# An image network on one core: layers 0 and 1 held as 4 rows x 32 channels, with the input turned by VectorE and the column transform first

## The reference, cut to what matters

```python
# layer 0: whole image moved down and right by (dy, dx), found from its own mean; cut at the border
offsets = clip(mean_feat @ W + b, 0, 28).astype(int32)
x = x + where(mask, gn(x)[b, i - dy, j - dx, :], 0)
# layer 1: 3x3 convolution of signs with summed signs of weights
x = x + conv(sign(gn(x)), sign(W).sum(axis=0), 'SAME') + b.sum(axis=0)
# layers 2 and 3: cosine transform along columns, real Fourier transform along rows, 32 x 32 modes kept,
# each mode times a 32 x 32 complex matrix R, and back; beside it a 32 x 32 channel matrix
v = einsum('kn,bcxn->bcxk', D, gn(x)); v = rfft(v, axis=-2, norm='ortho')[..., :32, :32]
u = irfft(einsum('ijab,ejab->eiab', R, v), n=224); v_out = einsum('kn,bcxk->bcxn', D, u)
x = x + relu(v_out + gn(x) @ W.T + b)
```

## Time and profile before

| | |
|---|---|
| median of 3 runs | 3808.79 us (3801.92 to 3814.15) |
| profiled execution | 3800.75 us, span 3798.7 us |
| TensorE busy, share of the span | 2990.2 us, 79% |
| VectorE | 2738.1 us, 72% |
| ScalarE | 1522.8 us, 40% |
| first stage (to the last instruction of its last image) | about 0 to 1818 us |
| mixing, layer 2 | 1820 to 1955 us |
| third layer | 1955 to 3085 us |
| mixing, layer 3 | 3085 to 3222 us |
| last layer | 3222 us to the end |

### The profile page before, as it was taken

How to read it: one execution, slowest core, us unless ns; L and a number is a source line. 1 busy time by engine, 2 the same in 40 slices (tenths; PEclk the granted TensorE clock), 3 DMA queues, 4 the chain that set the end, 5 groups by cost and what they waited for, 6 DMA issues and landing times. The chain is left out here.

```text
span 3798.7 us, 64095 instructions
## 1 busy us (share of the span) xinstructions
PE 2990.2 (79%) x20528; PEld 1622.4 (43%) x20528; DVE 2738.1 (72%) x4615; ACT 1522.8 (40%) x3060; POOL 36.9 (1%) x23
## 2 busy tenths in 40 slices
PE   2688888888888888888348787887878735999997
PEld 2455555555554555544243333333333315444443
DVE  2566666666566666665537889989898744899998
ACT  3477766666677766655312222222222213000000
POOL 0000000000000000000100000000000010000000
PEclk9799998999899998989658899898898965999998
DMA  4566765666666675653657757767576353999998
GB/s 121 160 196 191 207 203 169 183 177 187 173 194 177 199 207 169 184 163 110 137 150 222 234 196 224 219 213 226 191 243 192 141 120 103 345 387 386 383 386 296
DMA packets 244496, 793.86 MB, mean 209 GB/s; under 512 B 41706, under 2 KB 76190, under 8 KB 233396
## 3 DMA queue, kind: packets, MB, share of 16 engines
q1 hardware_dynamic: 172692, 473.01, 42.4%
q10 hardware_dynamic: 70912, 316.72, 23.7%
q0 software_dynamic: 608, 0.63, 0.1%
HBM read 464.31 MB, written 329.10 MB: 209 GB/s over the span
## 5 line engine op out<-in xcount | busy, mean ns | idle before, releaser
L1307 ACT ACTIVATE B_junk<-B_im,B_nk 128x896 bf16<-128x896 f32 x224 | 233.4, 1042 | 855.9 <-DVE B_im L1377 659.0
L1253 PE MATMUL B_ring<-B_im,B_wnorm 128*128 128x448 f32 x896 | 413.3, 605 | 157.7 <-DVE B_im L1347 155.9
L755 DVE SCALAR_TENSOR_TENSOR A_image<-A_cps,A_cbias,A_image 128x448 f32<-128x448 f32 x448 | 303.3, 681 | 226.8 <-PE A_cps L415 200.8
L1576 PE MATMUL C_ring<-C_im,C_wnorm 128*128 128x448 f32 x896 | 387.8, 571 | 24.4 <-DVE C_ubuf L1633 19.0
L415 PE MATMUL A_cps<-A_signa,A_cwa 128*64 128x448 bf16 x1344 | 354.1, 378 | 63.9 <-DVE A_signa L781 43.0
L373 PE MATMUL A_aps<-a_k_ident,A_tin 112*128 112x112 f32 x1792 | 274.8, 297 | 108.2 <-ACT A_image L525 72.3
L415 PE MATMUL A_cps<-A_signb,A_cwb 128*64 128x448 bf16 x1344 | 354.8, 378 | 0.0
L547 ACT ACTIVATE A_tout<-A_aps 112x512 f32<-112x512 f32 x448 | 242.4, 591 | 266.4 <-PE A_aps L426 266.1
L1253 PEld LDWEIGHTS B_ring<-B_im,B_wnorm 128*128 128x128 f32 x896 | 172.9, 204 | 402.7 <-issue 334.5
L1225 PE MATMUL B_ring<-B_rout,iB_k_rowf 128*64 128x512 f32 x896 | 269.3, 684 | 76.4 <-DVE B_rout L1370 76.1
L749 DVE SCALAR_TENSOR_TENSOR A_image<-A_sps,A_lin,A_image 128x448 f32<-128x448 f32 x448 | 304.4, 682 | 13.4 <-PE A_sps L373 3.2
(11 more groups left out here) (195 smaller groups left out, 4023.9 us busy)
## 6 DMA issues: line engine op xcount, KB each, us to landing
A_tin<-in_x SPq DMA_DIRECT2D x441, 448.0 KB, 4.9
B_rin<-x2s SPq DMA_DIRECT2D x1024, 112.0 KB, 3.4
x2s<-A_tout ACTq DMA_DIRECT2D x224, 448.0 KB, 4.4
x3s<-B_im ACTq DMA_DIRECT2D x112, 896.0 KB, 5.0
C_im<-x3s SPq DMA_DIRECT2D x112, 896.0 KB, 13.0
out<-C_rout ACTq DMA_DIRECT2D x192, 256.0 KB
out<-C_rout ACTq DMA_DIRECT2D x192, 192.0 KB
out<-C_rout ACTq DMA_DIRECT2D x64, 128.0 KB
```

What stands on the lines that cost most here:

```text
L755: nc.vector.scalar_tensor_tensor(out=dst, in0=cps[n % 2][:, 0:2 * SIZE].rearrange("p (j r) -> p j r", r=SIZE), scalar=cbias[par][:], in1=d ...
L1253: nc.tensor.matmul(slot(par, ("add", e))[:, lane % 2, 0:2 * SIZE], wnorm[par][:], im[par][:, EVN * e:EVN * (e + 1)].rearrange("p (m s) -> ...
L1576: nc.tensor.matmul(slot(add_place(e))[:, lane % 2, 0:2 * SIZE], wnorm[par][:], im[par][:, EVN * e:EVN * (e + 1)].rearrange("p (m s) -> p s ...
```

## The change

The mixing stages and the last layer stay as they are. In the third layer `turn_in`, its loads and its ring are gone; SP loads the image in seven DMAs of 896 KB in the form in which the first stage now leaves it, and PE waits for each group of eight row groups by itself.

The first stage is written anew:

- An image lies as 4 rows x 32 channels, rows in pairs, three buffers instead of two. Tiles are of 128 rows x 28 columns, 16 for an image (the second eight begin at row 96, so that 32 rows are loaded twice); each is loaded by four DMAs of 112 KB into `A_rin`, a ring of four.
- VectorE turns x's tiles straight into the image (`turn_x`, L789 of the changed kernel) and the shifted tiles into one buffer `A_moved` (L799), masks them (L805, L811) and adds them (L814). PE's L373 and ACT's L525 are gone. ACT sums and squares each tile of x instead (`sum_x`, `square_x`).
- Signs are written once (L842), in four pieces of 8 or 9 row pairs, into two small buffers. The convolution has 14 units of two row pairs; a unit has six bf16 matmuls of 128 x 128 with 448 columns (L460) and twelve small ones of 32 x 32, also 448 columns, for the rows above and below (L465, L467). VectorE adds a unit of 896 elements at a time (L820).
- The image is stored as it lies, seven DMAs of 896 KB. PE still turns it (L487) and ACT still copies it, now for the forward transform alone.
- The forward transform goes columns first (L501), then after a turn (L514) rows (L523), 64 x 64 with 128 columns each. There is one `colpart` buffer, so ACT's copy of piece k+1 waits for L523 of piece k. ACT copies the result (`copy_spec`), and SP stores it in eight DMAs with pieces of 128 bytes.
- A body has sixteen slots. Two lists set when tiles of x and shifted tiles are turned.

```diff
+        X_BY = [0, 2, 5, 7, 9, 11, 13, 14, 15, 16, 16, 16, 16, 16, 16, 16]
+        S_BY = [0, 0, 0, 1, 2, 3, 4, 6, 8, 10, 13, 16, 16, 16, 16, 16]
...
+            def load(flat, k, slot):
+                rows = flat.rearrange("(l f) c -> l (f c)", l=32)
+                for i in range(QG):
+                    first = i * SIZE + (k % 8) * CHQ
+                    sp.dma_start(rin[slot][32 * i:32 * i + 32, :],
+                                 rows[:, first * C:(first + CHQ) * C]).then_inc(in_full[slot], 16)
...
+                whole(0, 0)
+                whole(1, 0)
+                edges(0, 1)
+                whole(0, 1)
+                whole(1, 1)
+                edges(1, 0)
+                whole(0, 2)
+                whole(1, 2).then_inc(conv_full, 1)
...
+            def spectrum(b, k0, base):
                 for k in range(k0, k0 + 4):
+                    turn_spec(b, k, base + ring_t(k))
                     if k > k0:
+                        forward_rows(b, k - 1, base + ring_t(k - 1))
+                forward_rows(b, k0 + 3, base + ring_t(k0 + 3))
...
+            def copy_cols(b, k, seq):
                 act.wait_ge(a_full, seq + 1)
+                if k >= 1:
+                    act.wait_ge(col_read, b * 7 + k)
...
+            def turn_x(q, k, slot, loaded):
+                t, ch = divmod(k, 8)
+                dve.wait_ge(in_full[slot], loaded)
+                nc.vector.transpose(turned_view(image[q], SECOND * t, ch * CHQ, CHQ),
+                                    flat_view(rin[slot][:, :])).then_inc(tile_turned, 1)
+
+            def add_shifted(b, q, k, at_tile):
...
+                nc.vector.transpose(moved[:, :].rearrange("p (l q s) -> p q l s", q=CHQ, s=2),
+                                    flat_view(rin[at_tile % RING][:, :])).then_inc(tile_turned, 1)
+                dve.wait_ge(tile_turned, tile_no(b, at_tile) + 1)
...
-                        pe.wait_ge(turned_in, (b + 1) * 2 * CHUNKS)
                         pe.wait_ge(w_ready, b + 1)
+                    pe.wait_ge(in_full[par][k], (b - par) * 8 + 16)
...
-            def turn_in(b, par, ch):
...
+                    for k in range(GROUPS):
+                        load(b + 1, 1 - par, k)
```

More of the change, by code:

```diff
@@ L350, in _ @@
             body(0, True, False)
[L351 to L354 removed]
+            with sp.Fori(0, (NB - 4) // 3) as i:
+                for k in range(3):
+                    body(3 * i + 1 + k, True, True)
+            body(NB - 3, True, True)
             body(NB - 2, False, True)
@@ new lines, in turn_back @@
+            def turn_back(b, q, n):
+                pe.wait_ge(conv_added, UNITS * b + n + 1)
+                for half in range(2):
+                    seq = ring_base(b) + ring_o(b, n, half)
+                    ring_item(seq)
+                    for l in range(4):
+                        first = (2 * n + l // 2) * LPN + 2 * HR * half
+                        last = nc.tensor.transpose(aps[half][0:HR, l * P:(l + 1) * P],
+                                                   image[q][:, first:first + 2 * HR].rearrange("p (j s) -> p s j", s=2)[:, l % 2, :], con["k_ident"][:])
+                    last.then_inc(a_full, 1)
@@ L464, in forward_cols @@
+                cols = colpart[:].rearrange("p (c g y) -> p g c y", c=4, g=4)
+                side = slice(64 * (k % 2), 64 * (k % 2) + 64)
+                for g in range(4):
+                    last = nc.tensor.matmul(vps[side, P * (k // 2):P * (k // 2 + 1)], con["k_fwdr"][:, g, :], cols[:, g],
+                                            start=(g == 0), stop=(g == 3), skip_group_check=True)
                 last.then_inc(spec_full if k == 7 else col_read, 1)
@@ new lines, in body @@
+                    if has_x and s >= 13:
+                        statistics(b + 1, s - 12)
+            body(-1, 2, False, True, True, False)
+            body(0, 0, True, True, True, False)
+            with pe.Fori(0, (NB - 4) // 3) as i:
+                for k in range(3):
+                    body(3 * i + 1 + k, (1 + k) % 3, True, True, True, True)
+            body(NB - 3, (NB - 3) % 3, True, True, True, True)
+            body(NB - 2, (NB - 2) % 3, True, True, False, True)
+            body(NB - 1, (NB - 1) % 3, True, False, False, True)
@@ new lines, in body @@
+                    if has_x and s == 14:
+                        root(b + 1)
+                    if has_x and s == 15:
+                        lower(b + 1, (q + 2) % 3)
+            body(-1, 2, False, True, True, False)
+            body(0, 0, True, True, True, False)
+            with act.Fori(0, (NB - 4) // 3) as i:
+                for k in range(3):
+                    body(3 * i + 1 + k, (1 + k) % 3, True, True, True, True)
+            body(NB - 3, (NB - 3) % 3, True, True, True, True)
```

884 lines of the change are left out of this document (419 added, 465 removed).

## The result

| | before | after |
|---|---|---|
| median | 3805.36 us (4 runs) | 4200.62 us (4 runs, 4187.78 to 4212.11) |
| ratio | | 1.104, 95% interval 1.099 to 1.109 |
| profiled execution | 3800.75 us, span 3798.7 | 4212.11 us, span 4210.2 |
| first stage, to the mark | 1821.9 us | 2362.4 us (+540.5; forecast +67) |
| mixing, layer 2 | 133.8 | 132.2 |

What follows compares the result with a forecast made beforehand. It took TensorE to bound the first stage and VectorE the third layer. First stage +67, third layer -157, sum -90: 3711 us from the profiled 3800.75, 3715 with half of 8 us back; range 3570 to 3865.

Steps and rivals of the forecast that it cites:

- forecast +67: First stage as a whole: 1885 us against 1818 before, 67 us longer.
- Third layer, the start: Third layer, up to the first turn out: at 2003 instead of 2042.7, -39 us, bounds -26 and -45.
- Third layer, the body: Third layer, period of an image: 58.3 us instead of 66.7, bounds 54 and 62, a gain of 118 us.
- First stage, units 7 to 12: First stage, slots 7 to 11: VectorE's work is the limit, 38.5 us.
- So 2.9 for a unit: First stage, TensorE's time for a convolution unit: 2.9 us, the middle of 2.3 and 3.4.
- The rival that named these matmuls: First stage: small matmuls don't overlap and pay at each change, unit 3.6 us, period P = 114, total 3755; chance 0.10.
- The lull costs some 2.: First stage: TensorE works slower after its lull in slots 12 to 15, some 2 us a period.
- the 17: First stage, slots 12 to 15: statistics of the next two images, last two units, first signs and `lower`, 17 us.
- Slots 2 to 6, 32: First stage, slots 2 to 6: ScalarE 34 us, VectorE 31, some of ScalarE's finished later, so 32 us.
- The rival of the loads: First stage: late loads make it slower than before, 2.6 us a tile, period 121 us, total 3851; chance 0.20.
- VectorE idles 15: First stage, slots 0 and 1: of 22 us, VectorE has 7 us of work and idles 15.
- The ends: First stage, its four uneven pieces: 155 us to the first L831, then 95, 88 and 104.

Runs made afterwards that it cites:

- warm: The changed kernel with matmuls of unused result added behind each turn of slots 6 to 15 and around the statistics; 4204 us.
- noedge: The changed kernel without the twelve small 32 x 32 matmuls of each convolution unit; 3978 us.
- specpool: The changed kernel with the eight DMAs of the spectrum's store issued by GpSimd instead of SP; 4146 us.
- searly: The changed kernel with six of the sixteen shifted tiles moved into slots 0 and 1, the others one a slot behind them; 4032 us.
- planar: The changed kernel with signs stored in two planes a row pair, so convolution matmuls read and write PSUM contiguously; 4116 us.

## Why the prediction was wrong, step by step

The step that cost most is the convolution unit's term, 2.9 us where 3.8 was measured (7.1 at the low clock). The path through slots 2 to 6 and the ends of the stage were priced too low as well. The points in the order of the prediction:

- **Third layer, the start: right.** 37.1 us from the weights to the first turn out; 37 was the forecast.
- **Third layer, the body: mechanism right, size too good.** 58.3 was taken, 59.9 measured, within the 54 to 62 given. VectorE is busy 610 of 839.6 us and waits for TensorE; that they alternate was said. The last image is 2.7 us slower than its 56.0 of before and the end 2.9. So -128 instead of -157.
- **First stage, units 7 to 12: right.** 39.6 against 38.5, VectorE full.
- **"So 2.9 for a unit".** The bounds 2.3 and 3.4 were drawn from whole matmuls that write contiguously, with overlap as the only question. The rows of before hold no matmul that writes PSUM with a step, and the code did show one. Overlap was there, and the write halved the rate: 3.8, outside the bounds. The changes of kind, priced at 0.09 each and left out of the unit, make some 0.4 of it. Without the small matmuls the two stretches with TensorE as limit fall by 14.6 us. The rival that named these matmuls had a unit of 3.6, near the truth, for the wrong reason, and gave it P = 114, since it counted the high clock alone; at the low one a unit is 7.1.
- **"The lull costs some 2."** 0.74 of the clock in units 0 to 2 is some 6 us by warm's rows. In the last stretch noedge too lies above the 17.
- **"Slots 2 to 6, 32".** It was 42.7. Three terms were too small. VectorE's busy time was 34.3 and not 31 (signs at 4.41, and the statistics of the image before, which stood in no term). Its turns waited for loads, because SP spent 6.75 us on the spectrum's store; the store was costed as 5.5 us of DMA, of which the trace shows 1.9 (the 2 us that stood beside it and went unused was right), and never as time of SP's queue, behind which the loads stand (3.1 us of the stretch by specpool). All waits for loads are 5.1 us of this stretch, and the rest of them is open. And the stretch begins with TensorE still behind: in the body above, VectorE's addition of unit 3 waited 2.3 us for it.
- **The rival of the loads** had the right place in part (loads late in the middle of the body) but not the cause: halving the bytes gave 14 us, freeing SP's queue 54, and each left some 30 of the 42 us of waits for loads in the window.
- **"VectorE idles 15" in slots 0 and 1.** It idled 23.5 of 32.1. The prediction saw the hole and the full list behind it and drew no conclusion: stretches that lie one behind the other add up their limits, and work moved from a full one to an empty one is worth what it takes. That was worth 169 us in searly, where the small matmuls' pitch was worth 84 (planar) and the store's queue 54 (specpool).
- **The ends.** The four pieces that are no even period (up to the first L831, the next one, the last one, and the end behind it) took 552 us (166, 118, 120, 148) where 442 was forecast (155, 95, 88, 104): 110 over. Image 15 alone, with nothing but the convolution, took 148 us to the mark. In 78 of them VectorE waited for TensorE's units, and the last 31 are the end of the spectrum's chain.

Sum: 28.3 x 13 = 368, the ends 110, and 67 forecast make 545; less 4, since the forecast took the stage before to end at 1818 and the mark stands at 1821.9: the 541 measured. Shown by runs are the small matmuls and their cause, what moving the store off SP's queue gives, the signs' rate, the independence of the third layer and the worth of the lists. Not settled are the waits for loads that are left in units 2 to 7, the 1.5 us of units 12 to 0 that noedge leaves (18.5 against 17), and how much of the even period is TensorE's clock.

## What to carry to other kernels

Where a body's stretches have different limits, its time is the sum of the limits, not the busiest engine's share; look first for work that can move into a stretch where its engine idles. Price a matmul by where it writes as much as by its columns, and read the access pattern of each new one in the code before bounding it with rows of another. A DMA costs the queue that issues it as well as the engines that carry it: eight small ones held SP for 6.75 us ahead of the loads, while their data took 1.9 us of the sixteen engines.
